# Spreading the next head's preparation through the attention loop of an eight-core transformer layer

## What is computed

```python
x = x + attn(layernorm(x))
x = x + ffn(layernorm(x))
# attn: q = x@Wq.T ; kv = x@Wkv_down.T (64 wide) ; k = kv@Wk_up.T ; v = kv@Wv_up.T
#       softmax(q k^T / 16) v per head, then @Wo.T
# ffn:  (silu(x@wg.T) * (x@wu.T)) @ wd.T, weights int/127
```

## Time and profile before

| | us |
|---|---|
| median of 2 runs (1282.96 to 1283.8) | 1283.38 |
| the profiled execution's own time | 1281.81 |
| its slowest core, core 1, first to last instruction | 1280.3 |
| spans of the eight cores | 1274.3 to 1280.3 |

### The profile page before, as it was taken

One profiled execution on the slowest core, in us unless ns is written; L12 is line 12 of the kernel. 1 busy time (PEld: TensorE's weight loads), 2 busy tenths in 40 slices (PEclk: granted clock), 3 DMA queues, 4 the chain that ended last, 5 costly groups with the idle time before them and its releaser, 6 DMA issues.

```text
span 1280.3 us, 15712 instructions; the slowest of 8 cores (1274.3 to 1280.3 us)
## 1 busy us (share of the span) xinstructions
PE 1131.1 (88%) x5921; PEld 493.0 (39%) x5921; DVE 368.0 (29%) x682; ACT 417.5 (33%) x402; POOL 51.5 (4%) x102
## 2 busy tenths in 40 slices
PE   7647979888888988899899857999999999999998
PEld 3212525334342343423434212444444444444443
DVE  0573222532225321353215755010112210110122
ACT  0313646145550546406374322223210022322000
POOL 2000000000000000000000200000000020000000
PEclk9767575765757657675665677999999999999999
DMA  8940010100101010100100420222210082221122
GB/s 128 253 132 0 2 33 2 33 1 1 34 2 33 1 18 17 18 1 1 18 1 2 63 36 10 46 45 34 35 32 1 1 128 38 33 42 25 54 111 99
DMA packets 16410, 49.90 MB, mean 39 GB/s; under 512 B 1616, under 2 KB 1744, under 8 KB 14288
## 3 DMA queue, kind: packets, MB, share of 16 engines
q0 software_dynamic: 14144, 32.12, 15.9%
q1 hardware_dynamic: 2192, 16.78, 3.5%
HBM read 72.61 MB, written 8.39 MB: 63 GB/s over the span
## 4 chain that ended last, share of the span: by engine, by line
PE 77%; DVE 12%; ACT 5%; issue 3%; DMA 2%; DVEq 0%; ACTq 0%; POOL 0%; POOLq 0%
PE PA L179 22%; PE PB L179 21%; PE PC L179 18%; PE PD L179 16%; DVE x_fm L507 3%; DMA arena<-x 2%; ACT arena L434 2%; DVE arena L622 1%; DVE arena L624 1%; ACT arena L486 1%; DVE arena L362 1%; DVE arena L723 1%; ACT arena L527 1%; DVE arena L299 1%; PE PA L477 0%
## 5 line engine op out<-in xcount | busy, mean ns | idle before, releaser
L179 PE MATMUL PA<-arena 128*128 128x512 bf16 (+2 forms) x1088 | 316.5, 433 | 29.6 <-DMA arena<-x 9.6
L179 PE MATMUL PB<-arena 128*128 128x512 bf16 (+2 forms) x1152 | 295.3, 408 | 14.3 <-DVE x_fm L507 7.7
L179 PE MATMUL PC<-arena 128*128 128x65 bf16 (+3 forms) x2592 | 280.8, 281 | 25.8 <-DVE arena L624 16.8
L179 PE MATMUL PD<-arena 128*128 128x512 bf16 (+3 forms) x768 | 255.3, 467 | 30.8 <-DVE arena L321 10.8
L179 PEld LDWEIGHTS PC<-arena 128*128 128x128 bf16 (+2 forms) x2592 | 171.6, 125 | 189.5 <-issue 137.8
L434 ACT ACTIVATE arena<-PA 128x1024 bf16<-128x1024 f32 x128 | 131.1, 1024 | 214.2 <-PE PA L179 195.0
L179 PEld LDWEIGHTS PB<-arena 128*128 128x128 bf16 (+2 forms) x1152 | 117.3, 106 | 184.8 <-issue 77.6
L179 PEld LDWEIGHTS PA<-arena 128*128 128x128 bf16 (+2 forms) x1088 | 99.0, 100 | 164.4 <-issue 61.1
L434 ACT ACTIVATE arena<-PD 128x1024 bf16<-128x1024 f32 x128 | 131.1, 1024 | 60.8 <-PE PD L179 51.1
L179 PEld LDWEIGHTS PD<-arena 128*128 128x128 bf16 (+3 forms) x768 | 79.5, 108 | 173.3 <-issue 113.7
L821 DVE TENSOR_TENSOR arena<-arena 128x1024 bf16<-128x1024 bf16 x48 | 33.2, 692 | 301.9 <-ACT arena L812 301.9
(11 more groups left out here) (71 smaller groups left out, 322.6 us busy)
## 6 DMA issues: line engine op xcount, KB each, us to landing
x_fm<-x SPq DMA_DIRECT2D x1, 8192.0 KB, 42.7
out<-x_fm SPq DMA_DIRECT2D x8, 1024.0 KB, 3.9
arena<-wg POOLq DMA_DIRECT2D x24, 256.0 KB, 3.6
arena<-wu POOLq DMA_DIRECT2D x24, 256.0 KB, 3.4
arena<-wd POOLq DMA_DIRECT2D x24, 256.0 KB, 11.7
arena<-x POOLq DMA_DIRECT2D x1, 4096.0 KB, 30.8
arena<-wq POOLq DMA_DIRECT2D x8, 512.0 KB, 5.3
arena<-wo POOLq DMA_DIRECT2D x8, 512.0 KB, 5.1
```

The source lines that it names most:

```text
L179: e.matmul(o, l, r, start=st, stop=sp)),
```

## The change

The preparation of the next head moves into the current head's twelve steps: prepA after step (1,1), prepB after (1,3), prepC after (2,1), and the four Qp after (2,3), (3,0), (3,1), (3,2). The next head's block-0 Spairs move too: one after each of the four PVg of block 3, one after each UT, and the last two right after (even head) or between the WO2 (odd head). After an odd head four Spairs of block 1 are issued between the WO2 as well. No instruction is added or removed.

```diff
+        fill = {}
+        if nxt < H:
+            fill = {(1, 1): [lambda: emit_prepA(nxt)],
+                    (1, 3): [lambda: emit_prepB(nxt)],
+                    (2, 1): [lambda: emit_prepC(nxt)],
+                    (2, 3): [lambda: emit_Qp(nxt, 0)],
+                    (3, 0): [lambda: emit_Qp(nxt, 1)],
+                    (3, 1): [lambda: emit_Qp(nxt, 2)],
+                    (3, 2): [lambda: emit_Qp(nxt, 3)]}
         for j in (1, 2, 3):
             for i in range(4):
                 emit_Spair(h, j, 2 * i)
                 emit_Spair(h, j, 2 * i + 1)
                 emit_PVg(h, j - 1, i)
+                for f in fill.get((j, i), ()):
+                    f()
 ...
         emit_PVg(h, 3, 0)
+        if nxt < H:
+            emit_Spair(nxt, 0, 0)
         emit_PVg(h, 3, 1)
+        if nxt < H:
+            emit_Spair(nxt, 0, 1)
         emit_PVg(h, 3, 2)
+        if nxt < H:
+            emit_Spair(nxt, 0, 2)
         emit_PVg(h, 3, 3)
+        if nxt < H:
+            emit_Spair(nxt, 0, 3)
         emit_UT(h, 0)
+        if nxt < H:
+            emit_Spair(nxt, 0, 4)
         emit_UT(h, 1)
-        nxt = h + 1
+        if nxt < H:
+            emit_Spair(nxt, 0, 5)
         if h % 2 == 0:
-            emit_prepA(nxt)
-            emit_prepB(nxt)
-            emit_prepC(nxt)
-            emit_Qp(nxt, 0)
-            emit_Spair(nxt, 0, 0)
 ...
+            emit_Spair(nxt, 0, 6)
+            emit_Spair(nxt, 0, 7)
         else:
-            if nxt < H:
-                emit_prepA(nxt)
             ln2_xb = ln2_xsq = None
             for o in range(NCH):
                 emit_WO2(h, o, 0)
                 emit_WO2(h, o, 1)
                 if nxt < H:
                     if o == 0:
-                        emit_prepB(nxt)
-                        emit_prepC(nxt)
+                        emit_Spair(nxt, 0, 6)
                     elif o == 1:
-                        emit_Qp(nxt, 0)
 ...
+                        emit_Spair(nxt, 0, 7)
+                    elif 2 <= o <= 5:
+                        emit_Spair(nxt, 1, o - 2)
```

More of the change, by code:

```diff
@@ L655, in build_program @@
     for h in range(H):
+        nxt = h + 1
         emit_prepA(h)
@@ L678, in build_program @@
         emit_PVg(h, 3, 0)
+        if nxt < H:
+            emit_Spair(nxt, 0, 0)
         emit_PVg(h, 3, 1)
+        if nxt < H:
+            emit_Spair(nxt, 0, 1)
         emit_PVg(h, 3, 2)
+        if nxt < H:
+            emit_Spair(nxt, 0, 2)
         emit_PVg(h, 3, 3)
+        if nxt < H:
+            emit_Spair(nxt, 0, 3)
         emit_UT(h, 0)
+        if nxt < H:
+            emit_Spair(nxt, 0, 4)
         emit_UT(h, 1)
-        nxt = h + 1
+        if nxt < H:
+            emit_Spair(nxt, 0, 5)
         if h % 2 == 0:
-            emit_prepA(nxt)
-            emit_prepB(nxt)
-            emit_prepC(nxt)
-            emit_Qp(nxt, 0)
-            emit_Spair(nxt, 0, 0)
[L691 to L696, removed]
-        else:
-            if nxt < H:
-                emit_prepA(nxt)
+            emit_Spair(nxt, 0, 6)
+            emit_Spair(nxt, 0, 7)
+        else:
             ln2_xb = ln2_xsq = None
```

## The result

The changed kernel takes 1254.86 us (median of 11 executions) against 1282.89 (median of 10) beside it: 0.9797 of the time before, 95% interval 0.9771 to 0.9822. That is 28 us gained where 59 were forecast. The profiled execution took 1253.58 us. In some executions (four of the six of e4 and two of the four of e6 among them) the cores of one die or of both run at a lower clock for reasons outside the kernel; ratios here compare undisturbed executions only, medians include the others, and for e4 and e6 the profiled execution is given instead.

The account below looks back on a forecast made before the run. TensorE at a low clock was taken to bound the attention stage. Seven loops at +9.25 us, four even ends at -17.8, three odd ends at -15.5 and three heads at -2.1 sum to -59: 1224 us, range 1184 to 1270.

Parts of the forecast that it names:

- Term 1: Loop, next head's preparation (prepA, prepB, prepC): matmuls plus waits for PD, together 6.05 us a head.
- Term 2: Loop steps next to prepA or prepC: clock lifted for a step or two, -1.5 us a head (0 to -3).
- Step (3,3): Loop's last step: values group of block 3 waits for two exponentials, 2.8 us in all, -0.7 a head.
- Term 3: Even head's end, with the next loop's first two Spairs: 14.3 us against 32.1, a change of -17.8.
- the four pairs: Values group and Spair pairs at a head's end: 4.5 us at full clock, 7.3 at low, 5.9 taken.
- Rival 2: Loop: clock rises a Qp later, is lost in (3,3), prepA never lifts it; 1265 us, chance 0.18.
- The fourth rival: All attention runs at the full clock, which follows how busy TensorE has lately been; 1131 us, chance 0.04.

Follow-up runs that it names:

- e4: Changed kernel with score matmuls over 128 rows instead of 64, the upper 64 set to zero; ratio 0.9010, profiled execution 1155.47 us.
- e6: Changed kernel with the four Qp one step later, preparation in PB and zero-padded 128-row score matmuls; ratio 0.8722, profiled execution 1119.28 us.
- e2: Changed kernel with prepA, prepB and prepC of heads 1 to 7 computed in idle PB instead of PD; 1222.39 us, ratio 0.9520.
- e1: Changed kernel with its four Qp one step later each, after (3,0) to (3,3); 1241.91 us, ratio 0.9674.
- e8: Changed kernel with the next head's first two Spairs issued ahead of the first values group of block 3; 1232.07 us, ratio 0.9597.
- e7: Kernel before, in its old order, with score matmuls over 128 rows and zeros in the upper half; 1225.56 us, ratio 0.9552.
- e9: Changed kernel with Qp after (2,1), (2,3), (3,1), (3,3) and preparation after (1,0), (1,1), (1,3); 1238.11 us, ratio 0.9660.

## Why the prediction was wrong

**What held.** The bound (TensorE at the low clock), the direction, and most mechanisms of the forecast: the clock rises with the first Qp, the three steps after it start 3.44 us apart, the loop is slow up to there in most heads, projection steps are 1.7 apart at 0.50, odd ends take 41.9 to 42.2 (41.3). The steps that failed are three terms of the sum. The feed-forward stage kept its length.

**Term 1, the preparation: 6.05 a head, measured 7.8.** The working named the right waits, but undersized each. By the starts of the rows above, prepA begins 187.20 - 185.55 - 0.99 = 0.66 after the values group could be over (0.4 taken), occupies 189.02 - 187.20 = 1.82 (1.7 taken), and the Spair into PD starts 1.61 after the one into PA, 0.78 more than the plain 0.83 (0.5 taken). The old cost, 6.6, had been called the upper bound, and it was none: the waits there were others. Over seven heads about 12 us. e2 shows the term: with PB it is 4.1.

**Term 2, the lifted steps: -1.5 a head, measured about nothing on core 5.** Only head 0 was lifted behind prepA there, which gave 1 us. The waits of term 1 stand in the very stretch that was to lift the clock; with them gone (e2), it rose there in 42 of 56 loops instead of 9. They aren't the whole condition: on cores 0, 3 and 6 it rose behind prepA with the waits in place, and the loop of head 2 took 39.9 us there against 42.8 on core 5. About 10 us.

**The rest of the loops.** Step (3,3) took 3.15, not 2.8, 2 us over seven heads; the first Qp took 2.8 to 3.5 instead of 3.5, some 2.5 us back. Heads 2, 4 and 6 saved 2.6 us each, where 2.1 was taken: their first three values groups start 1.24 and 5.00 us apart, those of head 1 2.81 and 6.01. With that, 1.4 in all, the pieces come to 19 to 20 where the loops miss 19.

**Term 3, the even ends: 14.3, measured 17.1 four times over on the slowest core.** 12 us, in two halves. The first is a choice: the text said that it could not tell if the clock would survive the wait in (3,3), and took the middle of the four pairs, 5.9. On core 0 three of four even ends survived it, on core 5 none. The time is that of the slowest core, and eight cores differ by when their clock changes; in the executions compared the slowest took 1251.4 to 1263.0 us, and it was not always the same one. With the pairs at the low clock the sum gives 15.7, 1.4 more an end, 6 us in all. The second half is a size: at the low clock the pairs took 7.8 where the sum had 7.3 (their values groups start 1.96 us apart, not 1.82), and what follows took 9.3 (8.9 on core 0) where it had 6.7 + 1.7 = 8.4. e1 shows the cause of the loss: with the wait filled by a Qp, the four pairs of every even end on every core ran at the full clock; e8, with Spairs in it, kept it in 24 of 32.

Rival 2 had this piece (clock lost in (3,3)) and the missing lift behind prepA, and both came true, the first in even heads alone; its own first piece, a rise one Qp later, did not. Rival 2 without that piece is 1265 - 7 x 2.9 = 1245, and term 1's 12 us bring it to 1257, near the 1254.86 measured. Part of that nearness is luck: it counts 1.4 us in each of seven ends, and the loss was 2.8 in each of four.

**The fourth rival** is out for this kernel: in 47 of 56 loops the clock stays at 0.50 up to the first Qp. In e4 and e7 a loop of the same matmuls and columns, over 128 rows, ran at 1.00. The Trainium skill (TensorE: Matmul & The Clock Gate, "What's actually happening") has the clock follow how busy the engine has lately been. These traces agree that the clock moves with recent work, and differ in that busy time alone does not tell it; the measurement decides.

**Open.** Why odd heads kept the clock through the wait on all cores while even ones lost it on some, I can't say more than that it depends on when the clock last changed against the program. That e9's plain steps mostly kept the clock and those of the changed kernel behind prepA mostly didn't was not taken further. Nor was why the 64-row projection steps of e4 and e6 keep the clock in the odd ends (0.94 to 0.99) and not after the last head (0.50).

## What to carry over

Read the granted clock beside the busy time: a loop in which TensorE is always busy can still run at 1.2 GHz, and a contraction over 64 partitions is a reason; padding it with zeros to 128 cost 4 us at the start here and was still worth more than the whole reordering (0.9552 against 0.9797). When moving work into another loop, count which PSUM tile it uses and who holds that tile there, and give it an idle one. Where a gain depends on a clock that may or may not hold, on many cores, sum with the bad case, for the slowest core is likely to meet it, and price that case whole, what follows the stretch included.

## What was not expected of the hardware

- A loop of score matmuls over 64 rows and short values groups kept the clock at 0.50 with TensorE busy for 32.0 of 32.7 us; with the score matmuls over 128 rows, half of them zeros, it ran at 1.00 with TensorE busy for 18.6 of 26.5 (e7).
- A short wait can cost more than itself: 1.49 us ahead of the values groups cost a further 3.4 us (13.7 to 17.1) on the cores where the clock fell behind it.
- Eight cores with the same instructions differed by 15 us (1236.8 to 1252.0), 13.6 of it in the attention stage (487.8 against 501.4) with its different clock, and by 2.5 us when the clock mostly stayed up (e6).
- 16 matmuls of 65 columns take 0.99 us at 1.2 GHz and 0.62 at 2.4, less than a halving; 8 of 512 columns take 3.5 and 1.85.
